# First layer of a four-layer kernel: projection and convolution joined, bias on GpSimd, one decay buffer in SBUF, matmuls of zeros

## The reference, cut to what matters

```python
h = x * rsqrt(mean(x * x) + EPS) * rms_w
x1, g = split(h @ in_W + in_b)                 # 256 channels each
x1 = silu(conv(x1, conv_w, 4 taps, causal) + conv_b)
delta, B, C = split(x1 @ dbc_W + dbc_b)        # 16, 16, 16
delta = softplus(delta @ dup_W + dup_b)        # 256 channels
a[t, d, n] = exp(delta[t, d] * A[d, n])        # the decay, 16 states n
b[t, d, n] = delta[t, d] * B[t, n] * x1[t, d]  # the input
s[t] = a[t] * s[t - 1] + b[t]                  # the scan over 256 positions
y = silu(g) * sum_n(s * C)
out = y @ out_W + out_b + residual
```

## Time and profile before

| what | value |
|---|---|
| runs | 1680.04, 1689.86, 1689.90 us, median 1689.86 us |
| profiled execution | 1679.67 us, span 1677.9 us, mean granted clock of TensorE 0.853 |
| busy over the span | PE 1386.4, DVE 1273.9, ACT 1110.4, POOL 862.2 us |
| the first layer | 0 to 621 us of the span |

### The profile page before, as it was taken

How to read it: one execution, slowest core, us unless ns; L and a number is a source line. 1 busy time by engine, 2 the same in 40 slices (tenths; PEclk the granted TensorE clock), 3 DMA queues, 4 the chain that set the end, 5 groups by cost and what they waited for, 6 DMA issues and landing times. The chain is left out here.

```text
span 1677.9 us, 21483 instructions
## 1 busy us (share of the span) xinstructions
PE 1386.4 (83%) x6448; PEld 673.7 (40%) x6448; DVE 1273.9 (76%) x2157; ACT 1110.4 (66%) x1610; POOL 862.2 (51%) x1035
## 2 busy tenths in 40 slices
PE   4788888888888758999999468877788749999998
PEld 3344444444444323444444123333333314444443
DVE  2888787878778986788887488888888528888775
ACT  4766666655656634555555189999999945555554
POOL 5777666667666654555555433232323005555555
PEclk8989787877879988999999566778867669999999
DMA  6121111122111103322222000000000004322241
GB/s 211 64 89 51 50 51 50 52 67 83 50 50 50 51 0 136 151 119 101 101 101 101 0 1 1 0 0 0 0 0 0 1 30 173 114 107 107 111 165 53
DMA packets 27779, 110.88 MB, mean 66 GB/s; under 512 B 4033, under 2 KB 9554, under 8 KB 19282
## 3 DMA queue, kind: packets, MB, share of 16 engines
q1 hardware_dynamic: 27010, 110.15, 17.4%
q10 hardware_dynamic: 720, 0.15, 0.0%
HBM read 107.41 MB, written 2.88 MB: 66 GB/s over the span
## 5 line engine op out<-in xcount | busy, mean ns | idle before, releaser
L828 POOL TENSOR_TENSOR e_h_lo<-e_h,e_h_hi 128x512 f16<-128x512 f32 x272 | 315.0, 1158 | 272.4 <-ACT e_h_hi L944 261.3
L261 POOL TENSOR_TENSOR m_h<-m_b_sb,m_dx 128x512 f32<-128x512 f32 x256 | 319.6, 1271 | 177.4 <-POOLq L67 99.8
L631 DVE TENSOR_TENSOR_SCAN m_h<-m_decay,m_h 128x1024 f32<-128x1024 f32 x128 | 292.5, 2285 | 32.2 <-ACT m_decay L496 19.2
L360 PE MATMUL m_y_ps<-m_hc,ident 128*128 128x512 f32 x512 | 283.2, 681 | 0.0
L496 ACT ACTIVATE m_decay<-m_delta,mw_a_log 128x255 f32<-128x255 f32 x512 | 211.7, 461 | 83.4 <-DVEq L636 83.1
L1039 DVE TENSOR_TENSOR e_cu<-e_u,e_c_bc 128x512 f32<-128x512 f32 x256 | 176.0, 687 | 107.6 <-PE e_u L868 87.0
L939 ACT ACTIVATE e_g<-e_g 128x512 f32<-128x512 f32 x256 | 149.1, 582 | 163.2 <-PE e_g L868 163.2
L868 PE MATMUL e_g<-e_x_hi,ew_gate_up 128*128 128x512 f16 x544 | 210.4, 387 | 8.4 <-ACTq L943 8.4
L1444 DVE TENSOR_SCALAR a_d<-a_s 128x512 f32<-128x512 f32 x256 | 170.2, 686 | 56.7 <-PE a_s L1278 37.6
L868 PE MATMUL e_u<-e_x_hi,ew_gate_up 128*128 128x512 f16 x544 | 209.4, 385 | 0.0
L875 PE MATMUL e_y<-e_h_hi,ew_down 128*128 128x512 f16 x544 | 206.9, 381 | 1.6 <-POOL e_h_lo L828 1.6
(11 more groups left out here) (182 smaller groups left out, 2022.8 us busy)
## 6 DMA issues: line engine op xcount, KB each, us to landing
e_c_bc<-mix SPq DMA_DIRECT2D x64, 1024.0 KB, 6.7
m_b_sb<-b_rows SPq DMA_DIRECT2D x64, 512.0 KB, 5.4
ew_gate_up<-w_gate_up SPq DMA_DIRECT2D x1, 2176.0 KB, 13.5
out<-x_sb SPq DMA_DIRECT2D x8, 256.0 KB, 2.3
ew_down<-w_down SPq DMA_DIRECT2D x1, 1088.0 KB, 11.4
mix<-e_cT SPq DMA_DIRECT2D x16, 32.0 KB, 1.6
x_sb<-x SPq DMA_DIRECT2D x1, 256.0 KB, 2.9
mw_in_w<-w_in_w SPq DMA_DIRECT2D x1, 256.0 KB
```

Source lines behind the costliest of these rows:

```text
L261: ins = nc.gpsimd.tensor_tensor(h[:, m % 4, :, c], b_sb[:, p, 2 * m:2 * m + 2], dx[:, p, c:c + 1].to_broadcast([P, 2, T]), ALU.mult)
L360: ins = nc.tensor.matmul(y_ps[:], ident[:], hc[:, m % 2, n].rearrange("p c t -> p (c t)"), start=(m == 0 and n == 0), stop=(m == PAIRS - 1 ...
L631: nc.vector.tensor_tensor_scan(flat, decay[m % 2][:], flat, 0.0, ALU.mult, ALU.add).then_inc(scan_chain, 1)
L828: nc.gpsimd.tensor_tensor(h_lo[:, k], h[:, k], h_hi[:, k], ALU.subtract).then_inc(h_lo_ready, 1)
```

## The change

- **Projection and convolution joined.** The weights of the projection are multiplied beforehand by each of the four taps (`taps` is now 4 x 128 x 256, made on DVE in the prologue). The convolution then runs straight on the shifted `hT`, which has three zero columns ahead. `project_x`, `pad_x`, `xpad` and its semaphores go. The projection's bias goes into the bias of the silu (`x_bias`); for the first three positions, where fewer taps apply, one small matmul of 3 rows and 3 columns takes the surplus off (`ncorr`). `convolve(0)` moves to m 2 and `convolve(1)` to m 3, both behind the states. A new input `conv_rows`, 1280 numbers, is loaded broadcast to all partitions.
- **Output bias on POOL.** The bias matmuls of `project_out` go; POOL adds `out_b` to the residual instead (`add_bias`), in m 7 for the batch three ahead.
- **Decays.** Pair 0 has a buffer of its own in SBUF, `decay_head`; the other pairs take turns in the two PSUM tiles. ACT makes pair 0 of the next batch at m 6, before the silus, and pair 1 at m 7; `read_dbc` moves from m 1 to m 2.
- **Matmuls of zeros.** In pairs 1, 5 and 7 of every batch PE adds `ident16` times a float16 tile of zeros to `y_ps` four times, between `spread_c` and `add_states`.
- **Epilogue.** The float16 halves on DVE are made in three pieces, with `gate_y` and `update` between them.

```diff
-        hT = sb("hT", [P, 2, T])
-        xpad = sb("xpad", [P, DC, KC - 1 + T])
-        taps = sb("taps", [P, DC, KC, P])
+        hT = sb("hT", [P, 2, KC - 1 + T])
+        taps = sb("taps", [P, KC, DI])
+        early = sb("early", [KC - 1, KC])
+        ncorr = sb("ncorr", [KC - 1, DI])
+        x_bias = sb("x_bias", [P, 2, DC])
...
+        nothing = sb("nothing", [P, DC * T], FP16)
...
+        decay_head = sb("decay_head", [P, 2 * DC * T])
...
+        def decay_of(m, p):
+
+            return decay_head if m == 0 else decay[(m + p) % 2]
...
-                nc.gpsimd.memset(ones[:], 1.0)
+                nc.gpsimd.memset(early[:], -1.0)
+                nc.gpsimd.memset(nothing[:], 0.0)
...
-                c.link(nc.gpsimd.memset(xpad[:, :, 0:KC - 1], 0.0))
+                c.link(nc.gpsimd.memset(hT[:, :, 0:KC - 1], 0.0))
+                nc.gpsimd.affine_select(out=early[:], in_=early[:], compare_op=ALU.is_ge, fill=0.0, base=KC - 2,
+                                        pattern=[[-1, KC]], channel_multiplier=-1).then_inc(early_made, 1)
...
+            def add_bias(b):
+                take(pool, res_ready)
+                own = x_sb[:, bass.ds(b * TT, TT), :]
+                nc.gpsimd.tensor_tensor(own, own, out_b[:].rearrange("p (o d) -> p o d", o=1).to_broadcast([P, TT, DM]), ALU.add).then_inc(own_ready, 1)
...
                 norm()
+                add_bias(0)
+                add_bias(1)
...
+                    if m == 4 and first:
+                        add_bias(b + 2)
+                    if m == 7 and further:
+                        add_bias(b + 3)
...
-            def project_x(p, bank=t1):
-                take(pe, hT_ready)
-                for c in range(DC):
-                    ins = nc.tensor.matmul(bank[:, c * T:(c + 1) * T], in_w[:, c * P:(c + 1) * P], hT[:, p], start=True, stop=True)
-                ins.then_inc(x1_ready, 1)
-
             def project_g(p):
                 take(pe, t2_free)
                 for c in range(DC):
-                    ins = nc.tensor.matmul(t2[:, c * T:(c + 1) * T], in_w[:, (DC + c) * P:(DC + c + 1) * P], hT[:, p], start=True, stop=True)
+                    ins = nc.tensor.matmul(t2[:, c * T:(c + 1) * T], in_w[:, (DC + c) * P:(DC + c + 1) * P], hT[:, p, KC - 1:], start=True, stop=True)
                 ins.then_inc(g_ready, 1)
 
-            def convolve(c, bank=t1):
+            def convolve(c, p, bank=t1):
                 if c == 0:
-                    take(pe, xpad_ready)
+                    take(pe, hT_ready)
                 for k in range(KC):
-                    ins = nc.tensor.matmul(bank[:, c * T:(c + 1) * T], taps[:, c, k], xpad[:, c, k:k + T], start=(k == 0), stop=(k == KC - 1))
+                    nc.tensor.matmul(bank[:, c * T:(c + 1) * T], taps[:, k, c * P:(c + 1) * P], hT[:, p, k:k + T], start=(k == 0), stop=False)
+                ins = nc.tensor.matmul(bank[:, c * T:c * T + KC - 1], ncorr[:, c * P:(c + 1) * P], ident[0:KC - 1, 0:KC - 1], start=False, stop=True)
                 if c == DC - 1:
...
                     for c in range(DC):
-                        nc.tensor.matmul(t2[:, tt * DM:(tt + 1) * DM], yg[:, c, tt * P:(tt + 1) * P], out_w[:, c], start=(c == 0), stop=False)
-                    ins = nc.tensor.matmul(t2[:, tt * DM:(tt + 1) * DM], ones[:], out_b[0:1, :], start=False, stop=True)
+                        ins = nc.tensor.matmul(t2[:, tt * DM:(tt + 1) * DM], yg[:, c, tt * P:(tt + 1) * P], out_w[:, c], start=(c == 0), stop=(c == DC - 1))
...
+            def add_nothing(times):
+                for _ in range(times):
+                    nc.tensor.matmul(y_ps[:], ident16[:], nothing[:], start=False, stop=False)
+
             def prologue():
                 transpose_z()
-                project_x(0)
-                pe.sem_inc(z_read, 1)
-                project_g(0)
                 take(pe, zeros_made)
                 take(pe, taps_made)
                 for c in range(DC):
-                    convolve(c)
+                    convolve(c, 0)
+                pe.sem_inc(z_read, 1)
+                project_g(0)
                 transpose_z(y_ps)
                 project_dbc(0)
                 take(pe, bcd_ready)
                 project_delta()
-                project_x(1, y_ps)
+                for c in range(DC):
+                    convolve(c, 1, y_ps)
                 take(pe, pick_made)
                 take(pe, bc_ready)
                 spread_c(0, 0)
-                for c in range(DC):
-                    convolve(c, y_ps)
 
...
-                    if m == 4 and ahead:
-                        if first:
-                            convolve(0)
-                        convolve(1)
                     if m == 4 and not last:
                         project_g(1 - p)
                     if m == 6 and ahead:
                         project_dbc(p)
+                    if m in (1, 5, 7):
+                        add_nothing(4)
                     add_states(m)
...
-                    if m == (2 if first else 1) and ahead:
-                        project_x(p)
-                    if m == 3 and ahead and not first:
-                        convolve(0)
+                    if m == (3 if first else 2) and ahead:
+                        convolve(0, p)
+                    if m == 3 and ahead:
+                        convolve(1, p)
...
                 take(act, zT_ready)
-                nc.scalar.activation(hT[:, p], bank[:, 0:T], ACT.Copy, scale=rms_w[:, 0:1]).then_inc(hT_ready, 1)
-
-            def pad_x(bank=t1):
-                take(act, x1_ready)
-                for c in range(DC):
-                    ins = nc.scalar.activation(xpad[:, c, KC - 1:], bank[:, c * T:(c + 1) * T], ACT.Identity, bias=in_b[:, c:c + 1])
-                ins.then_inc(xpad_ready, 1)
+                nc.scalar.activation(hT[:, p, KC - 1:], bank[:, 0:T], ACT.Copy, scale=rms_w[:, 0:1]).then_inc(hT_ready, 1)
...
-                    ins = nc.scalar.activation(xs[:, p, c], bank[:, c * T:(c + 1) * T], ACT.Silu, bias=conv_b[:, c:c + 1])
+                    ins = nc.scalar.activation(xs[:, p, c], bank[:, c * T:(c + 1) * T], ACT.Silu, bias=x_bias[:, 1, c:c + 1])
...
-                        ins = nc.scalar.activation(decay[m % 2][:, at + 1:at + T], delta[:, p, c, 1:T], ACT.Exp,
+                        ins = nc.scalar.activation(decay_of(m, p)[:, at + 1:at + T], delta[:, p, c, 1:T], ACT.Exp,
...
-                pad_x()
+                take(act, bias_made)
                 normalise(1)
                 silu_x(0)
                 silu_gate(0)
@@ -508,35 +518,36 @@
                 read_dbc(0)
                 scale_hT(1, y_ps)
                 softplus()
-                pad_x(y_ps)
                 take(act, decay_zeroed)
                 take(act, delta_ready)
                 decays(0, 0)
+                decays(1, 0)
 
             def body(b, p, first=False, further=True, ahead=True, last=False):
                 for m in range(PAIRS):
-                    if m < PAIRS - 1 or not last:
+                    if m == 0:
+                        scanned.wait(-1, first)
+                        decays(2, p)
+                    elif 2 <= m < PAIRS - 1:
                         scanned.wait(m - 1, first)
-                    if m == PAIRS - 1 and not last:
+                        decays(m + 1, p)
+                    elif m == PAIRS - 1 and not last:
+                        scanned.wait(m - 1, first)
+                        decays(1, 1 - p)
+                    if m == PAIRS - 2 and not last:
                         take(act, delta_ready)
                         decays(0, 1 - p)
-                    elif m < PAIRS - 1:
-                        decays(m + 1, p)
                     if m == 0 and first:
                         silu_x(1 - p, y_ps)
                         exp_table()
-                    if m == (2 if first else 1) and not last:
+                    if m == 2 and not last:
                         read_dbc(1 - p)
                     if m == 2 and first:
                         normalise(b + 2)
                     if m == (4 if first else 3) and ahead:
                         scale_hT(p)
-                    if m == 4 and ahead and not first:
-                        pad_x()
                     if m == 4 and not last:
                         softplus()
-                    if m == 5 and first:
-                        pad_x()
                     if m == (7 if first else 5) and further:
                         normalise(b + 3)
                     if m == 6 and not last:
...
-                take(dve, res_ready)
+                take(dve, own_ready)
...
-                for d in decay:
+                for d in (*decay, decay_head):
...
-                for c in range(DC):
-                    for k in range(KC):
-                        ins = nc.vector.tensor_scalar(taps[:, c, k], ident[:], conv_w[:, c, k:k + 1], None, ALU.mult)
-                ins.then_inc(taps_made, 1)
```

(48 more changed lines are left out.)

## The result

The kernel after takes 1593.01 us in the median (1592.74 to 1594.13, four runs), the kernel before 1689.88 us beside it. The ratio is 0.9446, with an interval of 0.9406 to 0.9486. The profiled execution takes 1592.74 us with a span of 1591.0 us, 86.9 us less than that of before. One of the four runs of the kernel before took several times as long as the rest (6905.62 us) and is disturbed; the ratio leaves it out, and without it the median is 1689.86 us.

A forecast was written before the change was run, and what follows sets the result against it. DVE was taken as the bound, delayed by four waits of 87.8 us. Waits -78.7, lock +8, prologue +5 and epilogue -2 made -67.7 us, from 1679.67 to 1612 us; 8-in-10 range 1588 to 1655.

The forecast's parts named there:

- The waits of DVE and the floor of 30 us a batch: Steady stretch of the changed layer: DVE needs 30.3 us a batch, PE 26.8; batches fall from 36.6 to 31 to 32 us.
- The four waits: DVE's waits for c_ps (43.4 us), decays (19.2), softplus ahead of make_delta (18.1) and output ahead of update (7.1).
- The residues that I kept for short falls of the clock: Turn of the batch: 6 us of the c_ps waits and 1 us before update still paid.
- the first rival: Clock still falls at the turn of the batch; only 17 us gained, 1662 us; chance 0.15.
- all four waits vanish: Rival: DVE's four waits go entirely, no lock, prologue even; 1590 us; chance 0.1.
- its own forecast: Main case for the whole kernel: 1612 us, own range 1596 to 1640, chance 0.65.
- One chain, with the table loads at its head: Turn of the batch: ACT's table loads delay decays, PE idles, its clock falls, and all four waits follow.
- The rival in which they don't count as work: Matmuls of zeros on PE don't raise its clock and PE becomes the bound; 1741 us; chance 0.05.
- `pad_x`: Ahead of softplus on ACT: its 0.84 us and PE's projection make over half of each make_delta's 1.4 us wait.
- The scan of two SBUF tiles: Pair 0's scan and POOL lock each other out in SBUF; 0.5 us a batch, +8 us, ends 0 and +20.
- Prologue: First batch: larger conv_rows load, statistics and norm order, and two add_bias cost +5 us, ends -2 and +10.
- Epilogue: Layer's end: a piece of the 6.23 us operation fills DVE's 2.3 us wait before the last gate_y, -2 us.

The follow-up runs named there:

- u1: Kernel after without its matmuls of zeros: 1593.30 us, ratio 0.9489 to the kernel before.
- u2: Kernel after with the decays in the old order and two PSUM tiles, read_dbc in pair 1 again: 1592.74 us, ratio 0.9489.
- u12: Kernel after without the matmuls of zeros and with the decays in the old order: 1594.81 us, ratio 0.9505.
- b3: Kernel before with only projection and convolution joined and the epilogue in three pieces: 1628.31 us, ratio 0.9702.
- b4: Kernel before with only the output bias moved to POOL: 1627.69 us, ratio 0.9705.
- u3: Kernel after with projection, pad_x and a diagonal convolution apart as before: 1603.69 us, ratio 0.9554.
- u4: Kernel after with the output bias added by TensorE again, POOL still waiting for the residual without adding: 1612.68 us, ratio 0.9614.
- b1: Kernel before with only the matmuls of zeros added: 1659.97 us, ratio 0.9881.
- m1: Kernel after with the other two decay tiles in SBUF too, so every scan reads two SBUF tiles: 1761.74 us, ratio 1.0501.
- m3: Kernel after with conv_rows on its own semaphore and the first two add_bias in pairs 2 and 3 of the first batch: 1593.61 us, ratio 0.95.
- m7: Kernel after with conv_rows loaded last, first three add_bias in pairs 2 to 4, decays in the old order and tiles: 1591.02 us, ratio 0.9496.

## Why the prediction was right, and where it was not

**The waits of DVE and the floor of 30 us a batch** were right. The four waits made 87.8 us; 78.7 were forecast to go and 86.8 went. By term: decays -19.2 of -19.2; `make_delta` -17.7 of -16; `c_ps` -42.8 of -37.4; `update` -7.1 of -6.1. The residues that I kept for short falls of the clock are the first mis-sized term: the clock is at 1.00, and in u1, where it falls at five turns, DVE waits at none of them. That takes away the price of the first rival as well, 50 us for a clock that still falls.

**The rivals.** The prediction gave 0.1 to "all four waits vanish", 1590 us, and 0.65 to its own forecast with a range of 1596 to 1640. At 1593 us the result lies outside that range, and the trace shows what the rival said: all but 1.0 us of the waits gone and hardly a lock; only its even prologue is missing. The 8-in-10 range held because it took the rival in. The ends of the forecast's own terms, added up, would have given 1591 to 1643.

**"One chain, with the table loads at its head"** was wrong, though the sum didn't suffer. u2 and u12 have the old order of decays and wait 0.6 and 3.0 us for them. The decays were late because `silu_x` waited for a late convolution: ACT's idle time there goes where both repairs are in (u2), and stays with either alone (b3, b4). Two things made TensorE late, shown by b3, b4, u3 and u4: the path over `project_x`, `pad_x` and `convolve`, and the one-row bias matmuls in the midst of the turn, behind which the clock stays at half through `add_states` of pairs 0 and 1. I had priced the bias matmuls at their own time, under 1 us a batch; taken alone they are worth 49 us, and put back into the kernel after 19.7. That is the step that failed. That the sum came out in spite of it is luck: 56.6 of its 78.7 us (decays and `c_ps`) were to go mainly because early decays remove the idle time, and what removed them was two other parts of the same change. How one-row matmuls hold the clock at half is not shown, only that they do.

**The zeros** were rightly costed at nothing. They are not needed either. The rival in which they don't count as work is refuted by b1, where they raise the clock from 0.83 to 0.93, for 17 us (interval 0.9819 to 0.9944).

**Early decays** bring 32 us alone and nothing that can be told on top of the rest.

**`pad_x`** was right: in u3, where the clock is full, the path over `project_x` and `pad_x` costs 10.7 us, 6.6 of them the wait of `make_delta`; forecast was over half of 1.4 us in 14 batches. What `pad_x` costs without `project_x` was not run.

**The scan of two SBUF tiles** has the mechanism right and the size wrong: +8 forecast, 0.5 measured on DVE in the steady stretch (and 1.0 at the first scan, inside the prologue's 6.3). As argued, POOL mostly loses, some 2 us in fifteen of sixteen batches, and POOL has room. m1 shows what the lock costs where there is none: 11 us a batch. The Trainium skill ("SBUF — State Buffer", Who interferes with whom) is borne out for scans as well: the one that came second took longer, in the longest case POOL's input by 1.98 us (3.25 us for 1.27).

**Prologue** +5 forecast, +6.3 measured, for the reasons given and one more, the lock at the first scan. The runs took back 3.8 of it: 1.4 us by moving `add_bias` (m3), and with that, no lock and `conv_rows` last, 3.8 in all (m7). The other 2.5 us, with `statistics(1)` at 17.91 us instead of 14.26 among them, were not taken apart. **Epilogue** -2 forecast, 0.15 measured: the piece put into the gap is followed by one that waits 1.9 us for POOL. It is the same lock, which I had seen in the earlier trace rows and not applied there.

In sum, from -67.7 forecast: 8.1 more from the waits and 7.5 more from the lock, 1.3 less for the prologue and 1.9 less for the epilogue, make -80.1; measured are -86.9. Of the 6.8 us between, 6.0 are DVE's busy time in the steady stretch, which I had taken as fixed: it falls by 5.5 us, although it holds the 0.5 us of the lock, which the sum has already. Most of that is overlap: the durations of DVE's instructions there, added up by line, make 433.0 us before and 432.1 after, but their union makes 417.5 and 412.0. An instruction that waits for nobody starts a little before its forerunner has ended (54.31 + 1.20 = 55.51 us, the next at 55.42), and one that waits doesn't; so a wait that goes gives a little more than its length, 4.6 us in all here. The last 0.8 us are in the layer's end and the other layers, and I did not part them.

These are differences of two profiled executions. By the medians the change brings 96.9 us, because the profiled execution of before was 10 us under its median, and the prediction left open what parts them. The runs of the kernel before on all chips, the disturbed one left out, lie between 1661 and 1690 us, and the time goes with the mean granted clock: the fastest has 0.869, the slowest with a clock on record (1688.24 us) 0.839. The four of the kernel after lie within 1.4 us. So the spread is likely one of falls of the clock; no run shows why their number varies.

## What to carry to other kernels

A total of waits on the bound engine gave the time well, and the cause badly: before a wait is called the head of a chain, look at what its releaser itself waited for, in the idle time in brackets, and go on. Parts that each repair the same chain are not additive; measured alone they made 146 us, together 84, and only taking out a pair (u12) showed that the other two carry it. A matmul of one row, at the place where TensorE comes out of a gap, can cost many times its own duration.

## What the runs showed of the hardware

One-row float32 matmuls (two of them take 0.4 us to the start of the next row at full clock, 0.7 at half) behind a gap keep the clock down: with them it fell at eight of fourteen turns and behind them `add_states` took up to 3.78 and 3.62 us in two pairs running (u4); without them it fell at none (after), and where it fell, 3.24 was followed by 1.98 (u1). Matmuls of zeros keep it up: falls at five turns instead of fourteen (b1). A scan with both inputs in SBUF and a POOL operation that reads SBUF hold each other up: 2.28 us became 3.26, and 1.27 became 3.25. A broadcast load of 640 KB beside the other weights made all of them land 2.7 us later, and 2.0 us later when it was issued last.
